# Spreading the useful pieces between the row-maxima units of a transformer kernel's first part, five units earlier, loads by halves

## What is computed

```python
x = _layernorm(x + _L0_attn_ref(x, ...))   # causal attention, 16 heads of 8, q and k layer-normed per head
x = _layernorm(x + _L0_ffn_ref(x, ...))    # soft mixture: 8 experts x 64 slots
x = _layernorm(x + _L1_attn_ref(x, ...))   # delta rule, a scan over the 512 steps
x = _layernorm(x + _L1_ffn_ref(x, ...))    # gated MLP, 128-512-512-512-128

# soft mixture
logits = einsum('bsd,etd->bset', xn, se)
dispatch = softmax(logits, axis=1)
slots = einsum('bsd,bset->betd', xn, dispatch)
processed = gelu(slots @ w1) @ w2
combine = softmax(logits.reshape(b, s, e * t), axis=-1)
out = einsum('bnd,bsn->bsd', processed, combine)

# delta rule, one step
Sk = einsum('bhkv,bhk->bhv', Sm, ki)
Sm = Sm + bi * ki[..., :, None] * (vi - Sk)[..., None, :]
oi = einsum('bhkv,bhk->bhv', Sm, qi)
```

## Time and profile before

| | before |
|---|---|
| three runs, us | 1321.63, 1322.0, 1325.11 |
| median, us | 1322.0 |
| the profiled execution, us | 1320.49 |
| its span, us | 1318.7 |
| PE, DVE, ACT, POOL busy | 86%, 69%, 49%, 36% |
| mean granted TensorE clock | 0.938 of full speed |
| first part, to the first step of the scan | about 822 us |
| one slot of the loop (slot 5) | 85.33 us |

### The profile page before, as it was taken

The page is one execution under the profiler, slowest core; times in us unless marked ns, Lnnn a source line. Parts: engine busy times, 40 slices in busy tenths (PEclk is TensorE's granted clock), DMA queues, the critical chain, the costliest instruction groups (busy, mean ns, idle before and its releaser), DMA issues.

```text
span 1318.7 us, 19164 instructions
## 1 busy us (share of the span) xinstructions
PE 1137.4 (86%) x6056; PEld 603.7 (46%) x6056; DVE 908.6 (69%) x2097; ACT 641.3 (49%) x1258; POOL 480.9 (36%) x602
## 2 busy tenths in 40 slices
PE   5979889999898998989996851177999999999997
PEld 3434454553554544635444430133455555455453
DVE  3627537456588687786875577998799898898131
ACT  2161734726637457385373410333465556645642
POOL 3040311312334144252333243354537546556310
PEclk8989999899999999999899885588999999999999
DMA  4220110221322314124113058221020220200000
GB/s 116 71 90 32 49 64 10 74 73 35 113 67 69 111 33 146 42 49 134 47 37 73 20 143 204 69 51 37 22 67 17 51 67 8 58 24 8 25 9 8
DMA packets 86004, 79.84 MB, mean 61 GB/s; under 512 B 43056, under 2 KB 63664, under 8 KB 83888
## 3 DMA queue, kind: packets, MB, share of 16 engines
q1 hardware_dynamic: 85936, 79.01, 22.2%
HBM read 43.17 MB, written 35.00 MB: 59 GB/s over the span
## 4 chain that ended last, share of the span: by engine, by line
PE 60%; DVE 16%; issue 9%; ACT 8%; POOL 4%; DMA 2%; SPq 1%; ACTq 0%; DVEq 0%; POOLq 0%
PE ps L1348 15%; PE ps L1329 8%; PE ps L992 5%; PE ps L957 4%; PE ps L1031 4%; ACT arena L1482 3%; PE ps L995 3%; PE ps L1339 3%; PE ps L1002 3%; PE ps L1018 3%; ACT arena L1443 2%; DVE arena L1881 2%; PE ps L1060 2%; PE ps L1098 2%; PE ps L1080 2%
## 5 line engine op out<-in xcount | busy, mean ns | idle before, releaser
L1881 DVE TENSOR_REDUCE arena<-ps 128x4 f32<-128x512 f32 (+2 forms) x192 | 197.7, 1043 | 64.0 <-PE ps L995 60.9
L1348 PE MATMUL ps<-arena,late 128*128 128x512 f32 x512 | 227.1, 596 | 0.3 <-ACT arena L1631 0.3
L1443 ACT ACTIVATE arena<-ps 128x512 f32<-128x512 f32 (+2 forms) x200 | 110.4, 569 | 210.6 <-PE ps L957 99.0
L776 POOL TENSOR_SCALAR_AFFINE_SELECT arena<-arena 128x512 f32<-128x512 f32 x128 | 90.5, 710 | 265.9 <-ACT arena L1482 265.4
L1482 ACT ACTIVATE arena<-ps 128x1024 f32<-128x1024 f32 (+3 forms) x256 | 169.3, 713 | 31.0 <-PE ps L1018 29.7
L1348 PEld LDWEIGHTS ps<-arena,late 128*128 128x128 f32 x512 | 96.3, 192 | 114.4 <-issue 112.1
L1631 ACT ACTIVATE arena<-ps,f_s 128x512 f32<-128x512 f32 x128 | 83.3, 688 | 109.3 <-PE ps L1348 98.6
L1002 PE MATMUL ps<-mask_qk,ident_b 128*128 128x512 bf16 x388 | 103.9, 388 | 25.8 <-DVE arena L2165 25.8
L1443 ACT ACTIVATE arena<-ps,arena 128x128 f32<-128x128 f32 (+1 forms) x128 | 62.3, 528 | 120.6 <-DVE arena L1908 47.2
L957 PE MATMUL ps<-ident,arena 128*128 128x128 f32 (+1 forms) x624 | 102.2, 298 | 21.6 <-ACT arena L1443 12.6
L874 POOL TENSOR_TENSOR arena<-arena 128x256 f32<-128x256 f32 x128 | 93.5, 730 | 66.0 <-ACT e_w L1690 43.3
(11 more groups left out here) (187 smaller groups left out, 1941.7 us busy)
## 6 DMA issues: line engine op xcount, KB each, us to landing
qr<-q_rep SPq DMA_DIRECT2D x16, 512.0 KB, 5.0
kr<-k_rep SPq DMA_DIRECT2D x16, 512.0 KB, 5.9
scan_d<-late SPq DMA_DIRECT2D x56, 138.0 KB, 3.0
arena<-scan_d SPq DMA_DIRECT2D x12, 552.0 KB, 7.3
q_rep<-hilo SPq DMA_DIRECT2D x24, 256.0 KB, 3.2
k_rep<-hilo SPq DMA_DIRECT2D x24, 256.0 KB, 3.5
proj_d<-arena SPq DMA_DIRECT2D x8, 768.0 KB, 5.1
late<-proj_d SPq DMA_DIRECT2D x8, 768.0 KB, 4.4
```

The costliest lines, as they stand in the source:

```text
L776: g.affine_select(out=block, in_=block, compare_op=ALU.is_ge, fill=0.0, base=0, pattern=[[0, 4], [1, P]], channel_multiplier=-1).then_inc( ...
L1348: last = pe.matmul(ps[:, ring2.bank(f"{n}{c}"), :], w[:, k, c * P:(c + 1) * P], src[:, k, :], start=(k == 0), stop=(k == HC - 1))
L1443: return act.activation(dst, src(ps[:, bank, :]), func, **kw)
L1881: v.tensor_reduce(heads[:, 2 * pr:2 * pr + 2, gs[0]:gs[-1] + 1], ps[:, at:at + 2, 0:len(gs) * w].rearrange("p q (n w) -> p q n w", w=w), X ...
```

## The change

On TensorE, in slots that have a front and a mixture or a tail (1 to 6), five units stand earlier: x0 and x1 between the products of the last group, x2 before the turning of the last products, x3 and x4 before transpose_att. The pieces then stand one by one between the units (`AHEAD_TO`; without units ahead `UNITS_TO`), the two last combine blocks behind transpose_x1, with x16, x17 and x18 between and behind them. In slots with a mixture the idle matmuls between the units, before transpose_x1 and at the end are gone. VectorE reduces the five units at the matching places and gives `residual` the number already done. ScalarE loads the Exp table and takes x1T before it takes the combine result. Two of the shared banks change places.

SP loads q and k by halves: `load_half(b, 0)` waits for half of the scores only, and `store_heads` stands behind it, as a single DMA instead of eight; the last sequence counts on a semaphore of its own.

```diff
+X_AHEAD = 5
+X_AT = 16
+UNITS_TO = [2, 3, 5, 6, 8, 9, 11, 12, 13, 14, 16, 18]
+AHEAD_TO = [5, 6, 7, 8, 9, 10, 11, 12, 13, 14, 16, 18]
...
-        shared = [(F, "xT", 4), (T, "L0", 5), ...
+        shared = [(F, "xT", 7), (T, "L0", 5), ...
-        shared += [(hand, use, (7, 4, 5)[k % 3]) for k, (hand, use) in enumerate([
+        shared += [(hand, use, (7, 5, 4)[k % 3]) for k, (hand, use) in enumerate([
...
-                sp.wait_ge(p_ready, CREDIT + b * len(p_units))
-                for half in range(2):
-                    for j, dst in enumerate((qr, kr)):
...
+            def load_half(b, half):
+
+                if b > 0:
+                    sp.wait_ge(p_ready, CREDIT + (b - 1) * len(p_units) + (half + 1) * (len(p_units) // 2))
+                for j, dst in enumerate((qr, kr)):
+                    sp.wait_ge(split_stored[j], CREDIT + (b + 1) * 48)
...
             def store_heads(b):
                 heads_ready(b)
-                for t in range(N2):
-                    sp.dma_start(scan_d[t, bass.ds(b, 1), :, :].rearrange("o h w -> (o h) w"),
-                                 heads_of(b).out[t * NH:(t + 1) * NH, :]).then_inc(pre_stored, 16)
+                sp.dma_start(scan_d[:, bass.ds(b, 1), :, :].rearrange("t o h w -> t (o h) w"), heads_of(b).out) \
+                    .then_inc(pre_stored if b < B - 1 else last_stored, 16)
...
                 place_maxima(b, 1)
+                replicate(b + 1)
+                load_half(b + 1, 0)
                 if kept is not None:
                     store_heads(kept)
-                replicate(b + 1)
+                load_half(b + 1, 1)
...
+                            if x_ahead and gg == NG and jt in (1, 2):
+                                maxima_to(jt)
                 if moe is not None:
                     expert_hidden(moe, turn, 0)
-                chain_only = b is not None and moe is None and tail is None
+                if x_ahead:
+                    maxima_to(3)
...
                 if moe is not None:
                     expert_hidden(moe, turn, 1)
+                if x_ahead:
+                    maxima_to(X_AHEAD)
                 if b is not None:
                     transpose_att(b, turn)
...
+                pieces = [lambda j=j: project(tail, turn, j) for j in range(4)] if tail is not None else [None] * 4
+                pieces += [lambda n=n: expert_out(moe, turn, (n,)) for n in range(4)] if moe is not None else [None] * 4
+                pieces += [lambda t=t: combine(moe, turn, (t,)) for t in range(NT)] if moe is not None else [None] * 4
+                filled = moe is not None
+                for end, piece in zip(AHEAD_TO if x_ahead else UNITS_TO, pieces):
+                    maxima_to(end)
+                    if end == NM_AT + 1 and front is not None:
+                        transpose_maxima(front, turn, 0)
+                    if end == X_AT and b is not None:
+                        if front is not None and not filled:
+                            idle_matmuls(2)
+                        transpose_x1(b, turn)
+                    if piece is not None:
+                        piece()
                 maxima_to(X_LATE)
-                if front is not None:
+                if front is not None and not filled:
                     idle_matmuls(4)
...
+                if b is not None:
+                    act.activation(warm[:, :], ident[:, 0:1], ACT.Exp)
+                    take_x1(b)
+                if moe is not None:
                     take_combined(moe)
-                if b is not None:
-                    take_x1(b)
-                    act.activation(warm[:, :], ident[:, 0:1], ACT.Exp)
...
                 if b is not None:
+                    ahead = X_AHEAD if front is not None and (moe is not None or tail is not None) else 0
                     attend(b, 2)
+                    for k in range(min(ahead, 3)):
+                        maximum(front, f"x{k}")
                     attend(b, 3)
-                    residual(b, moe, front)
+                    for k in range(3, ahead):
+                        maximum(front, f"x{k}")
+                    residual(b, moe, front, ahead)
```

More of the change, by code:

```diff
@@ L561, in replicate @@
                 store_part(1, 1, 1)
-                sp.wait_ge(p_ready, CREDIT + b * len(p_units))
-                for half in range(2):
-                    for j, dst in enumerate((qr, kr)):
[L566 to L570, removed]
+            def load_half(b, half):
[3 more added lines that the diff above has]
+                    sp.wait_ge(split_stored[j], CREDIT + (b + 1) * 48)
+                    gs = slice(2 * half, 2 * half + 2)
+                    sp.dma_start(dst[:, gs, :].bitcast(F32),
+                                 (q_rep, k_rep)[j].rearrange("(g h) c d t -> (h c d) g t", g=NG)[:, gs, :]) \
+                        .then_inc(rep_loaded[half], 16)
             def place_maxima(b, h):
@@ L624, in _ @@
             replicate(0)
+            load_half(0, 0)
+            load_half(0, 1)
             load_x(1)
@@ L796, in scale_heads @@
                 if p is heads:
-                    g.wait_ge(pre_stored, CREDIT + held(b) * (N2 * 16))
+                    g.wait_ge(pre_stored, CREDIT + held(b) * 16)
                 g.tensor_tensor(p.kc, by_time(1), along(r_k), ALU.mult).then_inc(l_kb, 1)
@@ L1135, in early, with maxima_to @@
                     early_at += 1
+                chain_only = b is not None and moe is None and tail is None
+                x_ahead = b is not None and front is not None and not chain_only
+                x_at = 0
+                def maxima_to(end):
+                    nonlocal x_at
+                    while x_at < end:
+                        if front is not None:
+                            if chain_only:
+                                idle_matmuls(2)
+                            scores_for_maxima(front, f"x{x_at}", turn)
+                        x_at += 1
                 if front is not None:
@@ L1234, in slot @@
                     idle_matmuls(2, 0)
[L1235 to L1239, removed]
-                        if front is not None:
[L1241 to L1252, removed]
-                        expert_out(moe, turn, (2 * half, 2 * half + 1))
-                    maxima_to(8 + 2 * half)
-                for t in range(NT):
-                    if moe is not None:
-                        combine(moe, turn, (t,))
-                    maxima_to(11 + t)
-                if front is not None:
-                    transpose_maxima(front, turn, 0)
-                maxima_to(X_LATE - 3)
-                if b is not None:
-                    if front is not None:
-                        idle_matmuls(2)
-                    transpose_x1(b, turn)
+                pieces = [lambda j=j: project(tail, turn, j) for j in range(4)] if tail is not None else [None] * 4
[8 more added lines that the diff above has]
+                        if front is not None and not filled:
+                            idle_matmuls(2)
+                        transpose_x1(b, turn)
+                    if piece is not None:
+                        piece()
                 maxima_to(X_LATE)
-                if front is not None:
+                if front is not None and not filled:
                     idle_matmuls(4)
@@ L1749, in _ @@
             place_wv(0, 0, 1)
-            act.wait_ge(pre_stored, CREDIT + B * N2 * 16)
+            act.wait_ge(pre_stored, CREDIT + (B - 1) * 16)
+            act.wait_ge(last_stored, 16)
             act.wait_ge(sc_loaded[1], CREDIT + 48)
@@ L1931, in add_combined, with residual @@
                 v.tensor_tensor(y_moe, y_moe, x1, ALU.add).then_inc(moe_done, 1)
-            def residual(b, moe, front):
+            def residual(b, moe, front, reduced):
                 o = Order(v, dve_done, DVE1, b, CREDIT)
                 s = st
-                reduced = 0
                 def reduce_to(end):
```

12 lines of the change are left out of this document (6 added, 6 removed).

## The result

The changed kernel takes 1335.7 us (median; 1330.69 to 1341.93) beside 1323.51 us for the kernel before (1321.63 to 1332.95) run beside it: a ratio of 1.0075, 95% interval 1.005 to 1.010, worked out from all ten runs of each (the quotient of the two medians is 1.0092). The difference is under 1%, but its interval lies clear of 1. The forecast was 1323.5 us, the range 1301 to 1332.

A forecast was written before the change was run, and what follows sets the result against it. Engines handing over in turn, with TensorE setting the pace at a slot's end, were taken to bound slots 1 to 6. Terms -20.1 + 18.4 + 3.3 = +1.6 us on 1320.5, plus 1.5, gave about 1323.5 us; range 1301 to 1332.

The forecast's parts named there:

- what the spread pieces delay: Late combine blocks make GpSimd's scale_heads end 8.0 us into the next slot, holding VectorE's fold and TensorE: 18.4 us lost.
- The term of the stands: TensorE stands 4.6 us behind the late fold in each of slots 4 to 7: 18.4 us lost.
- The 1.0 us for a fold beside the score products: VectorE's fold, running beside GpSimd's score products, takes 2.72 us instead of 1.69, 1.0 more.
- the rule weighed there: VectorE and GpSimd lock a shared SBUF port pair per instruction: some 3 us in all, sum 8 us higher; not followed.
- the size of the clock: After TensorE's stands the clock falls in slots 4, 5 and 6 at slot 3's price: 3.3 us lost.
- rival 3: Each of four stands lowers the clock as long as in slot 2, 3.5 us each: 1334 us; chance 0.20.
- All of it lay on TensorE's path: Dropping 16 idle matmuls at 0.215 us each gains 3.44 us in each of slots 1 to 6.
- so no gain either: One store of the heads instead of eight gains nothing, as nothing in slots 1 to 6 waits for them on SP.
- the rest of the kernel as a block: After slot 7's attention the rest moves unchanged, so a microsecond gained or lost earlier is one of the total.
- The wait before transpose_x1: At a slot's end TensorE waits 1.1 to 1.2 us for xr; 1.1 us lost per slot.
- Loads by halves: SP loads the first half of q and k sooner, for the early units: no cost taken, bounds nothing and 3.4 us.
- rival 4: The first early unit stands for its load, up to 3.4 us in six slots: 1343 us; chance 0.03.

The follow-up runs named there:

- e1: The changed kernel with GpSimd doing scale_heads before add_combined: 1316.4 us, ratio 0.9954 to the kernel before.
- e4: The changed kernel with 17 idle matmuls (24 in slot 7) in TensorE's stand of slots 4 to 7, heads still late: 1328.0 us, ratio 1.0011.
- e7: The kernel before with only the 16 idle matmuls of each slot with a mixture left out: 1333.8 us, ratio 1.0086.
- e10: The kernel of e5 with all 16 idle matmuls per slot put back: 1325.9 us, ratio 1.0019.
- e6: The kernel before with only store_heads as a single DMA, at its old place: 1326.0 us, ratio 1.0036.
- e3: The changed kernel with store_heads as eight DMAs again, at its new place in SP's queue: 1332.5 us, ratio 1.0061.
- e5: The changed kernel with scale_heads ahead of the addition on GpSimd and store_heads as eight DMAs: 1314.65 us, ratio 0.9945 to the kernel before.
- e9: The kernel of e5 with no unit ahead between the last turnings: 1319.5 us, ratio 0.996.

## Why the prediction was wrong, point by point

**Right: the chain that decides.** The paragraph on what the spread pieces delay had L831 8 us behind x13 and scale_heads ending 8.0 us into the slot. x13 ended at 461.09, L831 started at 469.31 (8.2), and scale_heads ended at 475.65 + 1.35 = 477.00, 8.1 us into slot 5, which began at 468.92. The fold's wait was 3.69 us for 3.9. The wait of 1.18 us before the last turning of products became 0.42, as said. e1 shows the mechanism by taking it away. TensorE's timeline of after, that turning in slot 4 (and x0 ahead of it), x13 and the turning of x1:

```profile
435.55 0.44 PE L1002 MATMUL ps<-kr,qr 32*128 32x128 f32 x4
...
440.16 0.66 PE L967 MATMUL ps<-ident,arena 128*128 128x128 f32 x4 [0.42 <-ACT arena L1454]
...
460.70 0.39 PE L1005 MATMUL ps<-mask_qk,ident_b 128*128 128x256 bf16 x2
...
464.19 0.66 PE L967 MATMUL ps<-ident,arena 128*128 128x128 f32 x4 [0.58 <-DVE arena L1829]
```

**The term of the stands, near in sum.** Predicted 4 x 4.6 = 18.4; measured 3.73, 3.71, 3.73 and 6.07 = 17.2. The 1.0 us for a fold beside the score products was wrong in the slots 4 to 6 (L2004 took 1.89 us, not 2.72: GpSimd was late itself) and right in slot 7 (2.71, behind a wait of 4.23). On the rule weighed there (the Trainium skill, "SBUF — State Buffer", "SBUF: two separate sides", an exclusive lock for a whole instruction) the trace again bears out only a part: the three fold steps took between 0.2 and 1.0 us more beside GpSimd than the 1.69 of the earlier trace rows. The rule in full would give some 3, which is an estimate from products of about 1 us each.

**Failed: the size of the clock.** The step took slot 3's price of the earlier trace rows for three stands, 3.3 us in all, on the ground that dense work lies behind them. Measured: filling the stands alone gave 7.7 us back (e4), and by all runs the added low time cost some 9.5. The price was right, the duration was not: 1.10 us for the 3.4 us of low time in slot 3 is 0.32 us each, but the slots 4 to 6 had 27.3 us of it where the step took 10. Slot 4 fell to 1.2 GHz for 13.6 us, with TensorE fully busy. This was rival 3 for one slot in four, and half of it for the others; slot 7, which the step left out, had low time too (13.7 us against 6.8 before).

**Failed: "All of it lay on TensorE's path".** Most of the filler, 2.28 of 3.44 us, covered time of VectorE and xr. Taken out alone it gave 0.28 us at a slot's end (e7), not 3.44, and a lower clock. What the change gained it gained because useful blocks went into that time: 2.4 us in slot 3 at a like low time of 3.4 us (86.43 against 84.05), 1.8 to 2.5 per slot by e10, where 3.1 was predicted. The profile before had the number: the row of VectorE shown under e7, 1.01 us a reduction, beside units of 0.75 us on TensorE. Before filler was taken off at 0.215 us each, that comparison had to be made. The slots 1 to 3 together still gained 12.9 us (predicted 4.6 + 3.1 + 3.1 = 10.8), but slot 2's 6.5 hold a better clock: low time 13.6 us before, none after. That is partly chance, since e6, the kernel before with a single store, had 3.4 us of it there and took 86.8 us, 2.0 less than the kernel before in its trace.

**Failed: "so no gain either" for the single store.** It looked only at the chain of slots 1 to 6, and there nothing waits on SP. In the tail, where the last heads are stored, loaded and scaled one after the other, it costs about 3 us (e3 3.2, e6 3.65; e5 against e1 1.8; by the traces from xr of slot 7 to the scan, some 3). The forecast treated the rest of the kernel as a block, and the block grew by 4.9 us before the scan.

**Small and nearly right.** The wait before transpose_x1 was 0.6 us instead of 1.1, since xr came 3.0 us behind x13 and not 3.7: the copy before it took 1.12 us, not the 1.84 of the earlier trace rows. Loads by halves cost nothing: x0 began 14 us behind the issue of the first half of q; rival 4 had no ground. VectorE and SP in after:

```profile
463.01 1.12 DVE L1829 TENSOR_SCALAR arena<-arena 128x128 f32<-128x128 f32 x4
```

```profile
421.45 0.36 SPq L575 DMA_DIRECT2D qr<-q_rep  x1
```

Slot 1 gained 4.0 of the forecast's 4.6, at a low time of 6.8 us in both; how much of it the five units ahead gave is not shown (e9).

**The sum again**, on the span: slots 1 to 3 -12.9; in the slots 4 to 6 some -7.2 of gain (2.4 each, as in slot 3), 11.2 for three stands and by difference 7.9 for the clock; 7.0 in slot 7 (6.1 for its stand, 0.9 for the rest); 5.8 for the tail and the scan; 3.4 in slot 0: 15.2. Against the forecast's +1.6 the clock is 5.5 more (8.8 with slot 7's rest, for 3.3), the tail 5.8 and slot 0 3.4, which is chance; the stands are 1.1 less. The gain came to 20.1 us, the very figure that was forecast, but by luck: at 2.4 us instead of 3.1 in the plain slots it was short, and 4.1 us more than that in slot 2, with its better clock, made it up. Nearly all that was missed lay on the same side, and the upper end of the range, which stopped at half of rival 3, did not add it up.

**A version that beats both.** e5, the changed kernel with scale_heads ahead of the addition and with eight stores, takes 1314.65 us: 0.9945 of the kernel before (0.9919 to 0.9972).

## What to carry to other kernels

When useful work is moved to a later place, follow its result through every in-order engine that handles it: here a 1.27 us addition became the head of GpSimd's queue, and swapping two steps there was worth 16 to 19 us. Before filler is counted as a gain, ask which engine paces the stretch in which it stands; if it is another one, filler can be replaced by work, but taking it out gains little. The stands of 4 to 6 us on TensorE cost about half as much again in clock (17.2 and some 9 us), so both belong in the sum. And where many runs of a kernel are at hand with their granted clocks, the clock's share of a difference can be estimated from them, which one trace of each kernel can't give.

## What the runs showed of the hardware

- The issue of a small store on SP (beta, 32 KB) in the tail took 8.85 to 9.09 us in all six traces in which it came behind one 1.1 MB store (9.07 in after, 9.09 in e6), and 3.49 to 3.78 in all eight in which it came behind eight stores of 138 KB (3.68 before, 3.49 in e3). Why is not shown.
- Three stands of 3.7 us on TensorE went with 13.6, 6.8 and 6.9 us at 1.2 GHz in their slots, though TensorE was busy again at once; filling the one of slot 4 with idle matmuls kept the 10 us behind it at 2.4 GHz (e4).
- The same slot of the same program on TensorE can have a different clock: slot 1 took 82.5 us at a low time of 6.8 us in after and 87.1 at 17.1 in e3, which differ only in the store of the heads.
- Over the runs of any one kernel here, each us at 1.2 GHz went with 0.25 to 0.36 us of span.
- Without the filler of 16 short matmuls per slot the low time of the first part rose from 41 to 85 us (e7); with useful blocks in its place it was 55 (e5), and with the filler added to that it was 72 (e10). The mean granted clock over all runs of each kernel has the same order: 0.937 before, 0.922 in e7, 0.933 in e5 and 0.929 in e10 (medians). More activity on TensorE didn't always mean more clock.
